# A three-layer macaron kernel on eight cores: two base quarters before the expert outputs in the first pass, norms on GpSimd, write-backs queued later

## The reference

```
x = x + 0.5 * ffn(layernorm(x))          # pass "a"
x = x + attn(layernorm(x))               # scan, norm "b"
x = x + 0.5 * ffn(layernorm(x))          # pass "c", the same weights
```

## Time and profile before

| | us |
|---|---|
| time, median of 3 runs (lowest to highest) | 1209.45 (1207.55 to 1241.84) |
| the profiled execution's own time | 1212.14 |
| its span on the slowest core (core 1) | 1210.6 |
| spans of the eight cores | 1197.6 to 1210.6 |
| busy: PE, DVE, ACT, POOL | 931.9, 837.4, 769.9, 792.6 |

### The profile page before, as it was taken

The page is one execution under the profiler, slowest core; times in us unless marked ns, Lnnn a source line. Parts: engine busy times, 40 slices in busy tenths (PEclk is TensorE's granted clock), DMA queues, the critical chain, the costliest instruction groups (busy, mean ns, idle before and its releaser), DMA issues.

```text
span 1210.6 us, 22264 instructions; the slowest of 8 cores (1197.6 to 1210.6 us)
## 1 busy us (share of the span) xinstructions
PE 931.9 (77%) x7086; PEld 558.5 (46%) x7086; DVE 837.4 (69%) x654; ACT 769.9 (64%) x1834; POOL 792.6 (65%) x843
## 2 busy tenths in 40 slices
PE   2768954466768787977879996689979798895777
PEld 0333421222435555545555654466655465564333
DVE  2332245588866689986789996689987899998211
ACT  1240067799746786769767786888867787774300
POOL 1163221045865579896798999779999979888020
PEclk9888976798888798988889998799989998998889
DMA  9896997449998133452224444035735553553356
GB/s 194 160 166 94 167 198 169 116 90 195 193 222 238 44 106 105 139 159 70 95 99 140 157 158 149 19 97 190 219 107 148 175 192 98 182 179 102 100 174 213
DMA packets 51251, 176.00 MB, mean 145 GB/s; under 512 B 6268, under 2 KB 6720, under 8 KB 49984
## 3 DMA queue, kind: packets, MB, share of 16 engines
q1 hardware_dynamic: 41456, 139.82, 36.2%
q0 software_dynamic: 9680, 34.74, 18.7%
HBM read 184.08 MB, written 25.20 MB: 173 GB/s over the span
## 4 chain that ended last, share of the span: by engine, by line
PE 37%; ACT 16%; DMA 12%; DVE 12%; POOL 11%; issue 10%; POOLq 0%; SPq 0%; ACTq 0%; DVEq 0%
PE ps L488 10%; ACT da L771 9%; DVE hh L784 9%; DMA ring<-wts 8%; PE ps L508 7%; PE ps L412 6%; POOL ww L788 6%; PE ps L747 5%; PE ps L812 4%; ACT xlm L325 2%; DMA crep<-crow 2%; POOL diagb L842 1%; DMA ring<-wbf 1%; POOL vec L456 1%; DVE vv L447 1%
## 5 line engine op out<-in xcount | busy, mean ns | idle before, releaser
L784 DVE TENSOR_TENSOR_SCAN hh<-da,ps 128x1024 bf16<-128x1024 bf16 x288 | 645.2, 2270 | 116.3 <-PE ps L754 41.9
L788 POOL TENSOR_TENSOR ww<-hh,crep 128x1024 bf16<-128x1024 bf16 x256 | 543.4, 2125 | 99.0 <-DVE hh L784 87.4
L771 ACT ACTIVATE da<-dl,acols 128x255 bf16<-128x255 f32 (+1 forms) x1280 | 508.4, 474 | 95.4 <-DVE hh L784 94.7
L488 PE MATMUL ps<-ring,xlt 128*128 128x512 bf16 x1024 | 253.0, 386 | 12.2 <-DMA ring<-wts 10.4
L747 PE MATMUL ps<-diagb,dxt 128*128 128x256 bf16 (+1 forms) x1088 | 195.7, 295 | 63.7 <-DVE hh L784 60.9
L812 PE MATMUL ps<-identbS,ww 128*128 128x128 bf16 x2048 | 167.2, 228 | 7.2 <-POOL ww L788 3.8
L747 PEld LDWEIGHTS ps<-diagb,dxt 128*128 128x128 bf16 x1088 | 86.1, 101 | 143.0 <-issue 100.5
L508 PE MATMUL ps<-ring,ut 128*128 128x512 bf16 x512 | 135.0, 399 | 17.3 <-DMA ring<-wts 7.3
L488 PEld LDWEIGHTS ps<-ring,xlt 128*128 128x128 bf16 x1024 | 96.4, 99 | 111.9 <-issue 20.1
L412 PE MATMUL ps<-ring,xlt 128*128 128x512 bf16 x512 | 137.9, 415 | 5.3 <-DVE xlt L347 2.8
L812 PEld LDWEIGHTS ps<-identbS,ww 128*128 128x128 bf16 x2048 | 133.3, 102 | 12.1 <-issue 8.4
(11 more groups left out here) (91 smaller groups left out, 879.0 us busy)
## 6 DMA issues: line engine op xcount, KB each, us to landing
ring<-wbf SPq DMA_DIRECT2D x192, 512.0 KB, 5.5
ring<-wts POOLq DMA_DIRECT2D x64, 512.0 KB, 14.0
wbf<-ring SPq DMA_DIRECT2D x32, 512.0 KB, 10.2
x<-x_tm SPq DMA_DIRECT2D x9, 1024.0 KB, 10.4
out_tm<-x SPq DMA_DIRECT2D x32, 256.0 KB, 5.1
crep<-crow SPq DMA_DIRECT2D x16, 256.0 KB, 5.4
wxa<-WxTa POOLq DMA_DIRECT2D x1, 512.0 KB, 16.9
wdt<-WdT POOLq DMA_DIRECT2D x1, 512.0 KB, 19.4
```

Of the source, the lines that this page charges most:

```text
L488: t = E.op("tensor", lambda e, q=q, k=k: e.matmul(bank(b), X[:, k * P:(k + 1) * P], piece(n)[:, q * 512:(q + 1) * 512], start=(k == 0), st ...
L771: t = E.op("scalar", lambda e, q=q, n=n: e.activation(da[u % 3][:, q * T + 1:(q + 1) * T], dl[K % 3][:, 1:T], AF.Exp, scale=acols[:, k * N ...
L784: scan_tok[u] = E.op("vector", lambda e: e.tensor_tensor_scan(hh[u % 3][:], da[u % 3][:], ps[:, s * 1024:(s + 1) * 1024], 0.0, ALU.mult, A ...
L788: w_tok[u] = E.op("gpsimd", lambda e: e.tensor_tensor(ww[u % 5][:], hh[u % 3][:], crep[:, g * 1024:(g + 1) * 1024], ALU.mult), scan_tok[u] ...
```

## The change

1. In pass 0 the pieces come in another order (`ORDER`): the four base pieces of quarter 1 stand before the two expert pieces of quarter 0. The steps follow: base 0, base 1, experts 0, experts 1, base 2, experts 2, base 3, experts 3. The bank of a result is kept per tile and quarter, and seven PSUM banks are free in pass 0 instead of five.
2. The first half of A in pass 0 is interleaved over the three tiles instead of tile after tile.
3. The x tiles from 3 on are loaded only after the last A matmul of pass 0 (`tk["mid"]`).
4. The norm step is cut in three (`ln_fin`, `ln_root`, `ln_off`), and the routing's `pick` in two (`pick`, `mask`), a tick or two apart. The norms of tiles 1 and 2 for the scan and of tiles 5 and 6 for pass 2, eight halves in all, are computed on POOL instead of ACT; the second halves of tiles 3 and 4 move from ACT to DVE.
5. The scan's start is emitted in another order: only what unit 0 needs first.
6. The PE rates per tick go from 1.5 and 1.9 to 2.0 in chunk 0 and 1.4 after it; each tick's PE credit is raised by the DVE cost that the tick before spent; the cap goes from 2 to 4 rates.
7. Write-backs of pieces 40 on are queued 7 ticks after their load instead of 4, or just before the buffer's next load.

```diff
-PE_RATE = [1.5, 1.9, 1.9, 1.9, 1.9]
+PE_RATE = [2.0, 1.4, 1.4, 1.4, 1.4]
...
-                         tk.get(("xn", i - 8)))
+                         tk.get(("xn", i - 8)), tk["mid"] if i > 2 else None)
...
-        credit["pe"] = min(credit["pe"] + pe, 2 * pe)
+        credit["pe"] = min(credit["pe"] + pe + credit["more"], 4.0 * pe)
+        credit["more"] = 0.0
...
+                credit["more"] += d
...
+    ORDER = list(range(12)) + [14, 15, 16, 17, 12, 13] + list(range(18, NPC))
+    place = lambda p, n: p * NPC + (ORDER.index(n) if p == 0 else n)
...
-        s, p = q % RING, q % NPC
+        if NPC <= q - RING < 2 * NPC:
+            write_back(q - RING)
+        s, p = q % RING, ORDER[q] if q < NPC else q % NPC
...
-                defer(4, lambda: write_back(q))
+                defer(4 if q < NPC + RING else 7, lambda: write_back(q))
...
-    bank_free = [5, 6, 2, 3, 4]
+    bank_free = [5, 6, 2, 3, 4, 0, 1]
...
+        if (kind, i) in (("a", 0), ("a", 1), ("a", 2), ("a", 3), ("a", 4), ("b", 0), ("c", 7), ("c", 8)):
+            return ("scalar", "vector")[half]
+        if (kind, i) in (("b", 1), ("b", 2), ("a", 5), ("a", 6)):
+            return "gpsimd"
+        return "scalar"
...
+            if p == 0 and h == 0:
+                for i, q4 in ((0, 0), (1, 0), (0, 1), (1, 1), (2, 0), (2, 1)):
+                    s_a(i, h, q4)
+                for q4 in (2, 3):
+                    for i in tiles:
+                        s_a(i, h, q4)
...
-            route.append(step(lambda i=i: outer(i), need=[(("mix", p, i), 0)]))
-            route.append(step(lambda i=i: u_tr(i), pe=0.8, bank=True, need=[(("mix", p, i), 2)]))
+            route.append(step(lambda i=i: outer(i), need=[(("mix", p, i), 1)], name=("out", p, i)))
+            route.append(step(lambda i=i: u_tr(i), pe=0.8, bank=True, need=[(("out", p, i), 2)]))
...
+        if p == 0:
+            for what, jc in (("w", 0), ("w", 1), ("u", 0), ("u", 1), ("w", 2), ("u", 2), ("w", 3), ("u", 3)):
+                for q in range(4 if what == "w" else 2):
+                    for i in tiles:
+                        (s_w if what == "w" else s_u)(i, jc, q)
...
-    for q in range(4):
-        diag(0, q)
-    for K in (0, 1, 2):
-        prep_delta(K)
-    for K in (0, 1):
-        prep_dx(K)
-        prep_tr(K)
+    prep_delta(0)
+    prep_dx(0)
+    diag(0, 0)
+    diag(0, 1)
+    emit_da(0)
+    prep_tr(0)
     emit_bu(0)
-    emit_da(0)
+    prep_delta(1)
+    prep_dx(1)
+    diag(0, 2)
+    diag(0, 3)
+    prep_tr(1)
     emit_da(1)
+    prep_delta(2)
```

More of the change, by code:

```diff
@@ L198, in advance @@
             f()
-    credit = {"pe": 0.0, "dve": 0.0}
+    credit = {"pe": 0.0, "dve": 0.0, "more": 0.0}
     def pump(streams, pe, dve):
-        credit["pe"] = min(credit["pe"] + pe, 2 * pe)
+        credit["pe"] = min(credit["pe"] + pe + credit["more"], 4.0 * pe)
+        credit["more"] = 0.0
         credit["dve"] = min(credit["dve"] + dve, 2 * dve)
@@ L345, in ln_out @@
         src = o[:, 0:1024].rearrange("p (k t) -> p k t", k=8)
-        if by_vector(kind, i, half):
+        if half == 1 and norm_on(kind, i, 1) != "scalar":
             t = E.op("vector", lambda e: e.tensor_copy(dst, src), L["tr", kind, i, half], *after)
@@ L353, in ln_steps @@
     def ln_steps(kind, i, need, dst, free, need_dst=()):
-        out = [step(lambda: ln_fin(kind, i), dve=0.3, need=need)]
+        quick = norm_on(kind, i, 1) == "vector"
         fin = ("fin", kind, i)
-        out[0] = out[0][:5] + (fin,)
+        out = [step(lambda: ln_fin(kind, i), dve=0.3, need=need, name=("agg", kind, i)),
+               step(lambda: ln_root(kind, i), need=[(("agg", kind, i), 0 if quick else 1)], name=("root", kind, i)),
+               step(lambda: ln_off(kind, i), need=[(("root", kind, i), 0 if quick else 2)], name=fin)]
         for half in range(2):
-            out.append(step(lambda half=half: ln_norm(kind, i, half), need=[(fin, 1), (("xlm", half), 0), *need_dst],
+            out.append(step(lambda half=half: ln_norm(kind, i, half), need=[(fin, 0 if quick else 1), (("xlm", half), 0), *need_dst],
                             name=("nm", kind, i, half)))
@@ L361, in ln_steps @@
             out.append(step(lambda half=half: ln_tr(kind, i, half), pe=0.8, bank=True,
-                            need=[(("nm", kind, i, half), 1)]))
+                            need=[(("nm", kind, i, half), 0 if quick else 1)]))
             out.append(step(lambda half=half: ln_out(kind, i, half, dst(half), *free()),
@@ L391, in piece @@
         def piece(n):
-            return ring[(q0 + n) % RING]
+            return ring[place(p, n) % RING]
         def spent(n, i, tok):
@@ L396, in spent @@
             if left_of[n] == len(tiles):
-                freed[q0 + n] = tok
+                freed[place(p, n)] = tok
                 if p == 0:
@@ L414, in a_mm @@
                     start=(k == 0), stop=(k == 15)),
[L415 removed]
+                    *x_ready[kind, i], ring_tok[place(p, n)], bank_tok[b], sig=(q == 3))
             spent(n, i, t)
             S["a", i, h] = t
+            if p == 0 and h == 1:
+                tk["mid"] = t
             S["ab", i, h] = b
@@ L481, in w_mm @@
             if q4 == 0:
-                S["b", i] = take()
-            b = S["b", i]
+                S["b", i, jc] = take()
+            b = S["b", i, jc]
             n = 8 + jc * 6 + q4
@@ L575, in ffn @@
                         s_u(i, jc, q2)
+        for jc in range(4):
             for i in tiles:
@@ L595, in ln_for @@
                 if i > 2:
-                    out.append(step(lambda i=i: load_x(i), need=[(("a", 0, 2, 0, 3), 0)], name=("ld", i)))
+                    out.append(step(lambda i=i: load_x(i), need=[(("a", 0, 2, 1, 3), 0)], name=("ld", i)))
                 for c in range(4):
@@ L896, in build_nc @@
             todo.pop(0)()
-    while left([first, norms1]) or len(bank_free) < 5:
+    while left([first, norms1]) or len(bank_free) < 7:
         advance()
```

56 lines of the change are left out of this document (30 added, 26 removed).

## The result

| | us |
|---|---|
| before, median of 8 runs | 1210.45 (1206.34 to 1258.01) |
| after, median of 8 runs | 1217.29 (1213.20 to 1224.61) |
| ratio after to before | 1.0065, 95% interval 1.0035 to 1.0095 |
| profiled execution of after: own time, span (core 2) | 1224.61, 1223.1 |

By the bound of 2% this is no change; the interval says 0.35 to 0.95% slower. The forecast was 1158. Slow executions (two of the eight of before, one each of e3_rates_back and e4_all_three, two of the four of e9_before_routes) are left out of the ratios and of the times of the experiments, though not of the table, and e9 has no interval.

The account below looks back on a forecast made before the run. DMA engines were taken as the bound up to 200 us, with two holes, then idling where they could work ahead. Gains 15 + 22 + 4 + 8 + 2 = 51 us of span 1210.6 gave 1158; forecast 1140 to 1182, range 1130 to 1198.

Parts of the forecast that it names:

- First pass: Pass 0: DMA work alone would set it, piece 31 landing at 129 us and the pass ending at 135 against 153.7.
- both holes close: Pass 0: buffers freed ahead of the DMA engines' need, so the two stretches of lost DMA time, 19.4 us together, vanish.
- The start of the scan: Between pass 0 and chunk 0: new order worth 2 to 4 us, first scan about 149, mostly lost again at the x tile.
- Chunk 0: Chunk 0: about 50 steps against 29, 93 us of DMA from 182 on, chunk 1 beginning at 287 against 301.9.
- 12 us of coupling over the DMA floor: Chunk 0: allowance of 12 us added to the DMA floor of 275, giving 287 for the start of chunk 1.
- (a): Rival, the holes move: pass 0 gives 17 us, chunk 0 waits for pieces, chunk 1 keeps its stalls; 1192, chance 0.22.
- The norms on POOL: Eight norm halves on POOL: 2.3 us each, bounds 1.2 and 3.5, 18 us in all, lying beside other work.
- Chunk 1: Chunk 1: 29 us lost there before, 19 gained, 3 more for steps that left it; 203 us instead of 224.7.
- Chunks 2 to 4: Chunks 2 to 4: 2 us gain in each of 2 and 3, 8 us in chunk 4 with 64 steps against 85.
- (b): Rival, better coupling: chunk 0 near its floor of 275, chunks 2 to 4 5 us better each; 1130, chance 0.14.
- (c): Rival, half clock in the first pass: PE waits about 0.8 us for every piece, pass ends at 143; 1185, chance 0.06.
- (d): Rival, slower: POOL's ring reloads wait for write-backs in chunks 0 and 1, 24 at 4 us each; 1254, chance 0.08.

Follow-up runs that it names:

- e3: On after: PE rates, cap and credit put back as in before; 1210.42 us, ratio 1.0030 to before.
- e4_all_three: On after: the edits of e1, e2 and e3 together; 1198.02 us, ratio 0.9921 to before.
- e9: On before: only the routing of the three tiles of pass 0 laid side by side; 1198.14 and 1195.38 us, against 1206.0 for before.
- e1: On after: tiles 3 and 4 loaded together, their statistics wait until tile 2's expert vectors are done; 1221.79 us, ratio 1.0128 to before.
- e7: On e5: x tiles 3 and 4 loaded at the start again; 1194.01 us, ratio 0.9895 to before.
- e6: On e5: pass 0 routing side by side over three tiles, tiles 3 and 4 as in e1, without their quick norm order; 1180.21 us, ratio 0.9774 to before.
- e12: On e6: statistics of tile 5 may be laid 12 ticks after the tile's load instead of 3; 1162.94 us, ratio 0.9649 to before.
- e10: On after: the edit of e6 in the first pass, keeping after's rates and norms on POOL; 1194.31 us, ratio 0.9900 to before.
- e2: On after: the eight norm halves back on ACT, none on POOL; 1214.68 us, ratio 1.0063 to before.
- e5: On after: the edits of e2 and e3 without that of e1; 1199.40 us, ratio 0.9936 to before.
- e8: On before: only the PE rate of chunk 0 changed, 2.0 instead of 1.5; 1213.97 us, ratio 1.0056 to before.
- e11: On e6: after's credit scheme with lower rates (1.2 in chunk 0, then 1.4, cap 4); 1185.06 us, ratio 0.9823 to before.

## Why the prediction was wrong

**The failed step** is in First pass: "Base 1 before experts 0 puts 12 steps x 0.86 = 10.3 us of matmuls into the wait" and, from it, "both holes close". The steps did go into the wait, but the prediction took the wait as fixed. It was long because POOL's queue, in order, held ring loads of PE's steps ahead of tile 1's routing (e1), and with twelve more steps there the three starts moved from 79, 91 and 99 to 86, 102 and 109. The norms of the tiles that were held back had a smaller part in it (e7, 5 us). The prediction asked what is queued behind a waiting instruction for the write-backs only; it did not ask it of the ring loads that come with each step it moved. With the routing side by side (e6) the sum itself was good: piece 31 landed at 127.0 for a forecast of 129, the pass ended at 129.9 for 135, the x tile landed at 181.3 for 182. The end of A, taken as 47, came at 56.3 in after, since its interleaved order could only start at 33.8, behind the transposes of all three tiles; in e6 (55.9) that cost the sum nothing. The sum went by the row's 3.41 us a piece, and that is about what the DMA engines did when nothing held them. The Trainium skill, DMA: Bandwidth & Descriptors, Specifications, gave as an estimate some 16 us earlier than the forecast, about 119; e6, which has no hole left, did not come there (129.9).

**The start of the scan** was sized right: 14.6 us from the last matmul to the first scan in after, 14.9 in e6, 17.7 before, so 3 us for a forecast of 2 to 4. That most of an earlier start is lost at the x tile was right too: DVE waited 12.3 us for it in after, where the tile came late with the rest, and 21.4 in e6 for a forecast of 25. What the prediction took as given, that the statistics stand there, was worth 15 us more (e12).

**Chunk 0** ended at 330.5 for 287. Of the 43 us, 19 were inherited, since the x tile landed at 201.3 and not at 182. The DMA work from there on was 94 us for a forecast of 93, with 56 steps for 50. The term that failed is "12 us of coupling over the DMA floor": the idle time was 36 us in after, and in e10, where the tile landed by 182.2, chunk 0 still took 162.6. The 40 free microseconds of 200 to 260 in the earlier trace rows, which the prediction counted as room for the additional pieces, are not room: the DMA engines idle there because PE frees no buffer. In after and e10 it reads none until the expert vectors of pass 1 are there; in before it read none from 207 to 241 either, though there its next ring step was one of A, which waited for ACT's copy of a transposed norm. The higher rate does nothing for that. It puts its steps behind the hole, where the share is 0.91 to 1.00; PE waits 22 us for pieces in this chunk, 14 of them there. Rival (a), the holes move, named this: with the first pass cured and the rates kept (e10) the ratio is 0.990, and (a)'s 1192 of 1209 is 0.986. In after itself the first hole moved too, which (a) had not counted.

**The norms on POOL**, 2.3 us a half with a bound of 3.5: measured 3.78, outside the bound, and 30 us for the 18. Six of the halves (23 us) lie in chunk 0 and two in chunk 1. The line through 64 and 256 elements was drawn through instructions with f32 output; these write bf16. They were said to lie beside other work. Under the new rates that holds (e2), although PE's transposes wait 7.0 us for them in chunk 0; under the old rates they cost 11.4 us (e5 against e3).

**Chunk 1** took 208.0 for a forecast of 203, nearly right, but by another path. The 29 us said to be lost in it before were counted from nine units; DVE's timeline has eleven between 322.3 and 376.3, by which 23 are lost. That some 21 steps of PE "have left this chunk" is false: it has 92 steps, as before. The 28 additional steps of chunk 0 came out of chunks 2 and 3 (154 for 177) and chunk 4 (82 for 85), since the rate of 1.4 laid fewer there. Chunk 1 also got a new wait, in the timelines of SP and of POOL in after:

```profile
336.40 0.32 SPq L70 DMA_DIRECT2D ring<-wbf  x1
336.81 1.81 SPq L70 DMA_DIRECT2D crep<-crow  x4
```

```profile
331.54 0.18 POOL L827 COPY hlast<-hh 128x8 bf16<-128x8 bf16 x1
342.88 2.13 POOL L823 TENSOR_TENSOR ww<-hh,crep 128x1024 bf16<-128x1024 bf16 x1 [11.16 <-DMA crep<-crow]
```

The loads of C (`crep`) for chunk 1 stand in SP's queue behind the load of a bf16 piece of pass 2, which SP could issue only at 336.4, and the first product with C waited 11.2 us. In e3 SP issued the same loads at 268, before chunk 1 began:

```profile
268.35 3.32 SPq L70 DMA_DIRECT2D crep<-crow  x4
```

The wait is 11 us in e2 and 10 in e1 and e10, 1.1 in e3 and 2.8 in e8. How much of it reaches the time was not separated.

**Chunks 2 to 4.** Chunks 2 and 3 gained 12 us for a forecast of 4, because they had fewer steps. Chunk 4 lost 2 instead of gaining 8: that it would hold 64 steps was wrong (82; pass 7's share is counted in the tail), and in e8 13 fewer steps brought nothing, so its 15 us above DVE's busy time are not had by laying fewer of PE's steps there. The quick norms were to give 2 us in the tail; it is 3.4 to 4.4 shorter in the kernels e3 to e7 and e12, which have the old rates, and unchanged in after. The granted clock of the tail (medians over the cores) is 0.89 in those, 0.83 in after and 0.84 in e1, e2 and e10; whether that takes it back, or is only a sign of longer waits of PE, is open.

**The rivals.** (b) did not come; there is no better coupling, and the credit scheme at lower rates, with ten more steps in chunk 0, costs 6 us (e11). (c), half clock in the first pass, is not what cost the time: the granted clock is 0.90 for the pass in after, as it was (0.89; both count 0 to 37 as full, though four matmuls at 35.5 in after took 1.91 us), and it is 0.55 in 90 to 110, where PE stood for 8.3 and 3.3 us and had nothing to run. With the holes closed (e6) the mean clock of the first stage is 0.95, but the condition of the rival, a wait of 0.8 us for every piece, did not come: from 34 us on PE waited for a piece twice in the pass, 2.3 and 0.6 us. (Its sum was also too dear: an end at 143 for 135 would take 8 us, not the 27 from 1158 to 1185.) The Trainium skill, TensorE: Matmul & The Clock Gate, HAM oscillation, says that waits for DMA between groups of matmuls throttle the clock again. Behind the wait of 2.3 us in e6 it did fall, four matmuls later: the eight at 74.77 took 3.56 us, where eight at full clock take 1.89, and the granted clock is 0.72 in 74 to 80 and 1.00 in 80 to 90. In chunk 0 of after the trace agrees in part: behind five of the waits for pieces, of 1.5 to 5.6 us, four matmuls took 1.86 or 1.87 us, the lower level of 1.2 GHz, and behind the other two, of 2.3 and 3.3 us, 1.02 us, the upper one of 2.4 GHz. (d), POOL waiting for write-backs, did not occur: no ring load of POOL in after names a DMA as what it waited for. SP's queue did hold up other work, as (d) asked, but it was the loads of C. The late write-backs were never tried alone, nor was the interleaved first half of A.

**Where it came out.** The change without its rates and its norms on POOL (e5, 0.9936) is 8 us faster than before, where the parts left in it (first pass, start of the scan, quick norms) were to bring 19 of the 51 (17 at the x tile, 2 in the tail). The rates and the norms on POOL together then cost 16 us (1.0065 - 0.9936), 4 of them seen with the rates taken back alone and none with the norms alone; the two are not additive, and why was not separated. While the routing was one stream, the new order of pieces brought nothing with the x tiles held back (pass 0 ends at 151.4 in e5 for 152.6 before, medians over the cores) and 5 us with them loaded early (e7, 147.2), and 20 us lay in the routing's order and what e10 changed with it (e10 against after).

## What to carry to other kernels

Work that is pulled forward into a wait takes its whole trail with it (here each step of PE brought a ring load on POOL that waits for the step), so ask of a wait what its last link is, on which engine that link is queued, and whether the moved work now stands ahead of it there. Free DMA time is room only if buffers come free in it: a share near zero may mean that nobody can ask.
